# Gathered groups added one step later in the second and third pass of a graph network kernel

## The reference

```
x = x + L0(relu(layernorm(x)))   # for each edge: h[src] times the matrix of the edge's type, times a weight; summed by target
x = x + L1(relu(layernorm(x)))   # Chebyshev: Tx1 = prop(h), Tx2 = 2 prop(Tx1) - h, then relu(h W0 + Tx1 W1 + Tx2 W2 + b)
x = x + L2(relu(layernorm(x)))   # attention over each edge with 86 edge types, summed by target, plus a self loop
x = x + L3(relu(layernorm(x)))   # mean of h[src] by target
```

## Time and profile before

| | |
|---|---|
| time, median of 3 runs | 7773.39 us (7771.03 to 7800.02) |
| the profiled execution's own time | 7774.41 us |
| its span, first to last instruction | 7772.6 us |
| PE busy | 4872.0 us (63%) |
| DVE busy | 4897.8 us (63%) |
| ACT busy | 2357.4 us (30%) |
| POOL busy | 5242.6 us (67%) |
| mean granted TensorE clock | 0.640 |

### The profile page before, as it was taken

The page is one execution under the profiler, slowest core; times in us unless marked ns, Lnnn a source line. Parts: engine busy times, 40 slices in busy tenths (PEclk is TensorE's granted clock), DMA queues, the critical chain, the costliest instruction groups (busy, mean ns, idle before and its releaser), DMA issues.

```text
span 7772.6 us, 149728 instructions
## 1 busy us (share of the span) xinstructions
PE 4872.0 (63%) x41375; PEld 4126.7 (53%) x41376; DVE 4897.8 (63%) x16081; ACT 2357.4 (30%) x7420; POOL 5242.6 (67%) x5417
## 2 busy tenths in 40 slices
PE   5333333333337667677777776777777777786777
PEld 2222222222225555566666665677777776775666
DVE  5555555567778888866666665444444444449997
ACT  4444444430012222223544445211121212123322
POOL 2777777777747777757665662677777777756663
PEclk6555555555556776767776776555555555558998
DMA  7111111110012222224656666222222222214443
GB/s 171 14 14 14 14 14 14 14 14 13 13 22 53 52 52 52 52 44 143 213 190 203 201 198 205 59 41 41 41 41 41 41 41 41 41 34 94 100 100 79
DMA packets 464811, 547.95 MB, mean 70 GB/s; under 512 B 217753, under 2 KB 373945, under 8 KB 464629
## 3 DMA queue, kind: packets, MB, share of 16 engines
q0 software_dynamic: 173168, 146.14, 12.7%
q1 hardware_dynamic: 235013, 186.26, 9.4%
q10 hardware_dynamic: 56448, 213.62, 7.0%
HBM read 298.88 MB, written 246.72 MB: 70 GB/s over the span
## 4 chain that ended last, share of the span: by engine, by line
POOL 33%; DVE 21%; issue 18%; PE 17%; DVEq 8%; DMA 2%; ACT 1%; POOLq 0%; ACTq 0%; SPq 0%
POOL arena L712 33%; DVE tbuf L1813 6%; PE ps_agg L1112 6%; DVE tbuf L1806 3%; PE ps_agg L1239 2%; DVEq L1858 2%; DVEq L1561 2%; PE ps_wide L1223 1%; DVE msg L1857 1%; DVE H L1813 1%; DVE msg L1860 1%; PE ps_wide L1342 1%; PE ps_wide L1226 1%; DMA arena<-table,ibuf 1%; DVEq L1863 1%
## 5 line engine op out<-in xcount | busy, mean ns | idle before, releaser
L712 POOL DMA_INDIRECT arena<-table,ibuf x3328 | 3151.3, 947 | 1242.4 <-issue 1129.9
L712 POOL DMA_INDIRECT arena<-nodes,ibuf x2080 | 2088.6, 1004 | 1142.9 <-issue 616.2
L1112 PE MATMUL ps_agg<-mem_b,arena 128*32 128x80 f32 (+1 forms) x3744 | 457.6, 301 | 504.0 <-DVEq L1561 497.7
L1112 PE MATMUL ps_agg<-mem_a,arena 128*32 128x80 f32 (+1 forms) x3744 | 433.0, 291 | 533.0 <-DVEq L1561 511.0
L1112 PEld LDWEIGHTS ps_agg<-mem_b,arena 128*32 128x32 f32 (+1 forms) x3744 | 400.1, 152 | 554.1 <-DVEq L1561 520.9
L1112 PEld LDWEIGHTS ps_agg<-mem_a,arena 128*32 128x32 f32 (+1 forms) x3744 | 378.9, 146 | 592.6 <-DVEq L1561 528.9
L1813 DVE TENSOR_SCALAR tbuf<-iota,at_f 128x256 bf16<-128x256 bf16 x3185 | 680.9, 297 | 0.3 <-PE ps_t L1239 0.3
L1377 PE MATMUL ps_agg<-tbuf,msg 128*64 128x80 f32 x2496 | 373.6, 344 | 337.9 <-DVE msg L2039 337.9
L983 ACT ACTIVATE att<-score 128x8 f32<-128x8 f32 x208 | 43.3, 208 | 1649.1 <-DVE score L2030 1649.1
L1377 PEld LDWEIGHTS ps_agg<-tbuf,msg 128*64 128x64 f32 x2496 | 336.0, 227 | 359.0 <-DVE msg L2039 359.0
L835 ACT ACTIVATE tbuf<-O,tbuf 128x49 bf16<-128x49 bf16 x1664 | 448.5, 363 | 78.3 <-DVE H L1728 78.3
(11 more groups left out here) (388 smaller groups left out, 11745.8 us busy)
## 6 DMA issues: line engine op xcount, KB each, us to landing
table<-tbuf ACTq DMA_DIRECT2D x294, 544.5 KB
idx_a<-lows_d SPq DMA_DIRECT2D x637, 192.0 KB
arena<-table,ibuf POOLq DMA_INDIRECT x3328, 2.4
table<-tbuf ACTq DMA_DIRECT2D x98, 495.0 KB
arena<-nodes,ibuf POOLq DMA_INDIRECT x2080
table<-tbuf SPq DMA_DIRECT2D x25, 1024.0 KB, 4.3
idx_a<-lows_d SPq DMA_DIRECT2D x91, 224.0 KB
nodes<-O SPq DMA_DIRECT2D x7, 224.0 KB, 3.0
```

The source lines that it names most:

```text
L712: nc.gpsimd.indirect_dma_start(out=INTO[s][:, k, c, 0:WIDTH[s]], out_offset=None, in_=TABLE[s], in_offset=bass.IndirectOffsetOnAxis(ap=ibu ...
L1112: last = nc.tensor.matmul(ps_agg[ROW0[s]:ROW0[s] + CHN[s], 0:WIN], narrow[:, k, c, 0:CHN[s]], onehots[b][:, c, :], start=(c == 0), stop=(c ...
```

## The change

In VectorE's loop for s = 1 and s = 2 (`pick_weighed`) four things change. The addition of a gathered group moves one step later: group k from step 2k + 2 to step 2k + 3, the fourth from step 0 to step 1 of the next block. It stands ahead of the weighing of the next group in the same step. The block's sums are added, in both passes, behind the remainders of step 2 (in s = 2 they stood at the front of the step, in s = 1 behind the group's addition). Steps in which no group is weighed get a drain in the place of the weighing. TensorE's, ScalarE's, GpSimd's and SyncE's programs are as before.

```
--- before.py
+++ after.py
@@ -1843,8 +1843,6 @@
                     for q in range(NBATCH + ((8 if s == 2 else 4) if last else 0)):
                         if goes(q + 1):
                             compare_sources(i, f, q + 1)
-                        if s == 2 and q % NBATCH == 2 and (q >= NBATCH or not first):
-                            add_block(i, f + q // NBATCH - 1)
                         if q < NBATCH:
                             dve.wait_ge(s_got, count(i, f, q, 3))
                         if s == 2 and q % 4 == 2 and not first:
@@ -1873,14 +1871,16 @@
                             dve.wait_ge(s_mid, count(i, f, q, -1))
                             V.tensor_tensor(slot_rows[b][:, 0:n, 2 * D:SPLIT], by_tile(rest[b][:, 0:n * D]),
                                             slot_rows[b][:, 0:n, D:2 * D], ALU.subtract).then_inc(s_slot, 1)
+                        if q % NBATCH == 2 and (q >= NBATCH or not first):
+                            add_block(i, f + q // NBATCH - 1)
+                        if q - 3 in HIDDEN[s]:
+                            add_group(s, i, HIDDEN[s][q - 3], f)
+                        if q == 1 and not first:
+                            add_group(s, i, SLOTS - 1, f - 1)
                         if q - 1 in HIDDEN[s]:
                             weigh_group(s, i, HIDDEN[s][q - 1], f=f)
-                        if q - 2 in HIDDEN[s]:
-                            add_group(s, i, HIDDEN[s][q - 2], f)
-                        if q == 0 and not first:
-                            add_group(s, i, SLOTS - 1, f - 1)
-                        if s == 1 and q % NBATCH == 2 and (q >= NBATCH or not first):
-                            add_block(i, f + q // NBATCH - 1)
+                        else:
+                            dve.drain()
                         if s == 2 and q % 4 == 2 and (q >= 6 or not first) and q < NBATCH + 4:
                             next_pair(dve, i * TURN + (f + q // NBATCH) * TURN, made, end_pair)
                         if s == 2 and q % 4 == 2 and not first:
```

## The result

The changed kernel takes 7803.8 us (median of 12 runs, 7796.0 to 7818.4) against 7779.4 for the kernel before beside it (12 runs): ratio 1.003, 95% interval 1.0021 to 1.0040. The forecast was 7724 with a range from 7660 to 7800: both the sign and the range are wrong.

The account below looks back on a forecast made before the run. VectorE, busy 85%, was taken to hold the second pass; in the third, VectorE and TensorE wait for each other in turn. 7774.4 + 4 (second pass) - 54 (third) = 7724 us, range 7660 to 7800.

Parts of the forecast that it names:

- The fourth pass has its own steps: Fourth pass: its code is not touched by the change, so nothing was counted for it.
- (a): Third pass, from batch 6's send to TensorE's next wait: earlier target comparisons and the moved block addition leave -0.9 us.
- (d): Third pass, step 7: gets +0.74 us ahead of a TensorE pick; of (c) -1.0 us is left.
- R1: Rival, chance 0.22: in the third pass the waits only move; 25 x -0.5 = -13 us, 7765.
- (b): Third pass, step 4: its 2.36 us wait returns before step 5's target comparisons; counted 0.
- (c): Third pass, step 6: its 2.21 us wait goes and nothing else is late there; -1.7 us.
- The slow blocks: Third pass: six blocks with a slower second half, 54.7 us each, gain -3.1 us each, 19 us together.
- R2: Rival, chance 0.13: shorter TensorE pauses in the third pass keep its clock up, 2.2 us more a block; 7674.
- Second pass, +4: Second pass: 19.1 us of waits and 17.3 us of idle time go, 40.6 us for 104 pairs is added.
- the 17.3 us before L1827: Second pass: idle time before the block's addition falls from 0.79 to 0.10 us, 25 x 0.69 gained.
- R4: Rival, chance 0.05: the new drain costs 0 in place of 0.31 us in 104 even second-pass steps; 7692.
- R3: Rival, chance 0.13: slower, VectorE's odd-step weighings and comparisons come 0.74 us later; 27 us third pass, 23 second; 7824.

Follow-up runs that it names:

- e10: Changed kernel with never-run drains, 112 behind the second pass and 108 behind the third (third pass's loop 128, fourth's 256 instructions on); 0.9967, 7764.1 us.
- e6: Kernel before with the group and block additions moved in the third pass alone, 108 never-run drains behind it; 0.9960, 7760.1 us.
- e2: Changed kernel with 92 never-run drains behind the third pass, so the fourth pass's loop lies 128 instructions on; 0.9990, 7781.0 us.
- e1: Kernel before with 36 never-run drains behind the third pass, so only the fourth pass's loop lies later; 1.0026, 7810.6 us.
- e12: Kernel before with 80 never-run drains behind the third pass; 1.0018, 7810.9 us.
- e3: Kernel before with only the block's additions moved behind the remainders in both passes, no drain added; 1.0007.
- e7: Kernel before with the second pass's reduction of picked rows adding two of three parts, so less VectorE work; 1.0006, second pass 1028.6 us.
- e8: e2 with the second pass's reduction adding two of three parts, as in e7; 0.9991, second pass 1030.7 us.
- e4: Kernel before with only the groups' additions one step later, their drains, and 92 never-run drains behind the third pass; 0.9993, 7784.2 us.
- e11: Kernel before with both moves in the second pass alone, 112 never-run drains behind the third pass (third pass's loop 16 instructions on); 1.0007.
- e9: e6 with 16 of its 108 never-run drains moved behind the second pass, so the third pass's loop lies 16 instructions on; 0.9990, 7783.2 us.
- e15: e6 with 48 of its 108 never-run drains moved behind the second pass (third pass's loop 48 instructions on); 1.0084, 7858.5 us.
- e16: e6 with 80 of its 108 never-run drains moved behind the second pass (third pass's loop 80 instructions on); 1.0126, 7894.8 us.

## Why the prediction was wrong

A good place of a loop is in this table one at which its pass was shortest: shifts of 0 and 128 instructions, give or take the four of the third pass's first block, and for the fourth pass 256.

| pass | unchanged code of the pass (the fourth: at good places), us | changed, loops at good places | changed, as it is | predicted |
|---|---|---|---|---|
| second | 1020.0 to 1031.5 (8 profiles) | 1030.7 (e10) | 1031.2 | +4 |
| third | 1281.0 to 1285.3 (5) | 1251.5 (e10), 1248.3 (e6) | 1277.5, e2 1281.1 | -54 |
| fourth | 675.7 to 683.4 (13) | 682.4 (e10) | 701.2 | 0 |

**"The fourth pass has its own steps".** This is the step that failed first. It is true of the code, and the pass still lost 25 us (forecast 0), since its loop came to lie where it has to be fetched anew in every turn; e1 makes that loss with nothing else changed, e2 takes it back. The prediction counted the new drains as time of VectorE and never as length of a program. The trace of before held the hint: 129 packets on that queue, none in the steady passes. The Trainium skill, "Runtime: NRT & Kernel Launch", section "Instruction fetch mechanics", says that most engines hold two blocks of 256 instructions, and that a taken branch to a target outside them waits for a fetch. A turn of the fourth pass's loop is 330 recorded VectorE instructions here (three blocks of 108, 105 and 117) and one of the changed third's 286, code that is not executed not counted; so an estimate from that page is that each fits at some places and touches a third block at others. The runs agree: shifts of 0 and 128 (for the fourth also 256) fetch nothing in the steady part, 36, 48 and 80 fetch five packets a turn. The runs also give the price: 14 to 22 us in the fourth pass, against 679.9, the middle of the 13 profiles at good places, and 92 to 124 in the third, against e6. It is not a price per packet, since e1 and e12 fetch the same number and differ by 7 us.

**Third pass, steps (a) to (d), -1.9 a block.** The starts of L1823 give the periods. At equal place, ordinary blocks (49.5 to 52.5 us) went from 51.15 to 51.02 us (e10): of 1.9 us 0.1 came. For these blocks this is R1, and it is the second step that failed. The wait for L1112 became one for the send: in the changed kernel

```profile
4123.75 1.46 DVE L1813 TENSOR_SCALAR H<-iota,at_f 128x256 bf16<-128x256 bf16 x7 [1.56 <-PE ps_agg L1239]
...
4132.11 0.42 DVE L1823 TENSOR_TENSOR big<-big,ps_agg 32x256 f32 x1 [0.40 <-issue]
...
4141.27 0.25 DVE L1580 TENSOR_TENSOR big<-big,ps_agg 32x80 f32 x1 [1.04 <-issue]
4141.80 0.42 DVE L1554 TENSOR_TENSOR arena<-arena,ew_s 128x256 f32<-128x256 f32 x1 [0.29 <-issue]
...
4151.06 1.33 DVE L1813 TENSOR_SCALAR H<-iota,at_f 128x256 bf16<-128x256 bf16 x6 [2.75 <-PE ps_agg L1239]
```

Step (b) was right. Step (c) was wrong in taking TensorE's idle time behind it as won: its wait for L1806, 172.2 us, is still 162.8 in the changed kernel, and from the first to the last addition of a block it is 167.1 before and 165.3 in e10, where some 120 were forecast. Step (a) left out that L1580 in step 3 now follows the block's additions, so that its load, so far behind a wait, is bare: 1.04 us in nearly every block.

**The slow blocks, -3.1 each.** Here most of the gain is. From the kernel before to e10 the pass is 29.5 us shorter. Six blocks over 52.5 us, 55.0 in the mean, become one of 54.0, which is some 20 us of it; the five short blocks went from 46.8 to 45.4 us, 6.7 in all, and the ordinary ones give the rest. In the five profiles of the unchanged code 6 to 10 blocks are slow, in e6 none. The forecast had 19 us for its six slow blocks, so the number is close, but by luck: it came from the wait for the last send before L1823, and that wait falls from 24.7 to 1.1 us in e3 and in the changed kernel too, where 7 and 8 blocks are still slow. The count was off as well: it has 17, 6 and 3 blocks, 26 where there are 25 periods, of which 14, 6 and 5 are ordinary, slow and short.

The gain goes with the clock, as R2 had it, at some half of R2's size: in the kernel before the clock is at its lower level, by its records, for 34 to 39 us of a slow block and 24 to 27 of an ordinary one, and over the pass its mean rises from 0.73 to 0.76. That the clock is the cause is not shown, since no run holds it apart from the waits, and e3 speaks against the clock alone: it is at the lower level for 602 us of the 25 periods, as e10 is for 605 (the kernel before for 683), and yet takes 1275.4 us. At 16 instructions further on 6 to 8 blocks over 52.5 us are back and the clock is at 0.73 to 0.75.

**Second pass, +4.** The size is about right, but by luck, since two errors met. "VectorE is the late one" was wrong: rows 2 showed GpSimd without one wait for a slot, which fits an engine that sets the pace, and I read it as slack. e7 and e8 show that it does. So the 17.3 us before L1827 could not come as a gain, and only what lifts VectorE above the gathers' 41.2 us costs: the groups' half alone does, with 42.1 to 42.8 us a block and 1047 us, and there GpSimd does wait for slots, 13.1 us between 2390 and 3380 (e4), and with the block's half VectorE is back at 41.6, level with them. Inside the block the forecast holds: idle before L1827 falls from 19.6 us to 0.6, TensorE's wait for it from 58.2 to 13.2, and L1554, which had no idle time, has 0.3 to 0.4 each time:

```profile
DVE arena L1554 <- issue: 33.0, 94, 0.4
DVE msg L1858 <- issue: 33.0, 188, 0.2
DVE tbuf L1806 <- issue: 26.9, 95, 0.4
...
DVE arena L1554 <- DMA arena<-nodes,ibuf: 1.3, 2, 0.7
```

R4 (a free drain) cannot be told from these, since the gathers hide it. The gathers themselves are a little slower, (783.7 + 239.9) / 787 x 32 = 41.6 us a block, as they are in e7 without the change; why stays open:

```profile
L712 POOL DMA_INDIRECT arena<-nodes,ibuf x787 | 783.7, 996 | 239.9 <-issue 234.5 <-ACT ibuf L826 5.5
```

**In sum.** Profile against profile the three passes give +11, -3.5 and +25.5 us, 33 of the 34.7 between the two profiled executions (7774.4 and 7809.1). One profile of the kernel before is a low base, though. Against the middle of the profiles of the same code (1028, 1283.8 and 679.9 us) it is +3 in the second pass; in the third -32 at a good place and +26 by its place; and +21 in the fourth by its place: +18, where the medians show +24.4. The rest is within what one profile differs from the next. R3's slower side came, and not by R3's mechanism. With both loops at good places the change is worth 0.33%, half of what was forecast. That figure belongs to these places: 16 instructions further on the changed third pass takes 1269.5 to 1281.1 us and the unchanged one 1281.8 (e11), and at 48 and 80 the unchanged one was not run.

Open: why a shift of 16, with no packet fetched in the steady third pass, costs 18 to 33 us. The first differences in a block are small (0.19 us of idle between the block's first and second addition L1823 in place of 0.07, and in the pass 19.6 us of waits before the pair's sums in e9 where e10 has 3.0), and the clock is low for longer, 647 us against 605. The unchanged third pass with the same shift (e11, 1281.8) loses nothing. No run separates the cause from its effects.

## What to carry to other kernels

An instruction added to a program moves every loop of its engine behind it. Look at the instruction packets in the steady part of each loop before and after a change, first of all where an untouched stage got slower, and try a pad in a branch that is not taken: in this kernel the place of two loops was worth more than the edit, and without e2 and e10 the edit would have been thrown away as slower.

An engine with an unbroken stream of issues that never waits for a buffer may be the one that sets the pace, as GpSimd was here beside a VectorE that was busy 85% of the time; take work away from the suspect before you price its edits.

In a stage in which two engines wait for each other in turn, a wait removed need not pay by its own length: in this third pass the ordinary blocks gained 0.1 us each, and most of the gain came from slow blocks that were no longer slow.

## What the runs showed of the hardware

- An instruction packet is 8192 bytes. The fourth pass, with 330 recorded VectorE instructions a turn, took 676 us without and 701 with 45 packets in its steady part; the changed third, with 286, took 1248 without and 1340 with 103. It was five packets in a turn at each of the bad places (e1, e12, e15, e16). The largest holes stand before L1806, were up to 1.5 us long in the fourth pass and up to 4.4 in the third, and the profile calls them "issue".
- Sixteen instructions that never run moved the third pass by 21 us (e6 1248.3, e9 1269.5), without a packet in its steady part.
- The same second pass took 1020 to 1032 us in eight profiles, with a granted clock of 0.72 in the shortest and 0.69 in e1 and e6: a difference of 11 us in that pass between two profiles says nothing on a change.
